# Four-layer graph network: head aggregation in transposed form, straight code, another order

## What is computed

```
h = relu(layernorm(x));  x = x + L0(h): softmax over leaky_relu((h W1)(h W2)^T), masked; times h W3; relu
h = relu(layernorm(x));  x = x + L1(h): graph attention, 4 heads of 64; elu
h = relu(layernorm(x));  x = x + L2(h): the one that the change rewrites:
        Q = h Wq + bq; K = h Wk + bk; V = h Wv + bv        4 heads of 64
        scores = Q K^T / 8, -inf where adj == 0; attn = softmax(scores)
        out = (attn V) Wo + bo; layernorm(out) * gamma + beta
h = relu(layernorm(x));  x = x + L3(h): graph attention, other weights; elu
```

## Time and profile before

| | us |
|---|---|
| median of 3 runs | 3187.79 |
| lowest and highest of them | 3183.66, 3192.85 |
| the profiled execution | 3183.85 |
| its span, first to last instruction | 3182.1 |
| mean granted clock of TensorE, as a share of 2.4 GHz | 0.985 |
| busy: PE, DVE, ACT, POOL | 3035.8, 2168.6, 1629.6, 765.6 |

### The profile page before, as it was taken

The page is one execution under the profiler, slowest core; times in us unless marked ns, Lnnn a source line. Parts: engine busy times, 40 slices in busy tenths (PEclk is TensorE's granted clock), DMA queues, the critical chain, the costliest instruction groups (busy, mean ns, idle before and its releaser), DMA issues.

```text
span 3182.1 us, 85495 instructions
## 1 busy us (share of the span) xinstructions
PE 3035.8 (95%) x35494; PEld 2287.4 (72%) x35494; DVE 2168.6 (68%) x5660; ACT 1629.6 (51%) x3457; POOL 765.6 (24%) x917
## 2 busy tenths in 40 slices
PE   4799999999999999999999999999999999999985
PEld 2577777777777777777777777777777777777754
DVE  3467767766767766767766767766766766766764
ACT  1355455455555545555545555545555545555533
POOL 1222222222222222222222222222222222222221
PEclk8999999999999999999999999999999999999998
DMA  3000000000000000000000000000000000000000
GB/s 75 14 8 9 15 15 15 8 15 9 15 15 16 8 15 8 16 15 15 9 15 8 15 15 15 8 15 9 15 15 16 8 15 8 16 8 8 2 8 14
DMA packets 38468, 43.75 MB, mean 14 GB/s; under 512 B 2496, under 2 KB 37312, under 8 KB 38048
## 3 DMA queue, kind: packets, MB, share of 16 engines
q1 hardware_dynamic: 37552, 36.97, 3.7%
q0 software_dynamic: 496, 0.92, 0.3%
HBM read 21.11 MB, written 16.78 MB: 12 GB/s over the span
## 4 chain that ended last, share of the span: by engine, by line
PE 90%; ACT 4%; DVE 3%; issue 2%; POOL 0%; SPq 0%; DMA 0%; DVEq 0%; POOLq 0%; ACTq 0%
PE ps L895 19%; PE ps L1000 16%; PE ps L901 11%; PE ps L1051 8%; PE ps L931 7%; PE ps L1026 7%; PE ps L952 7%; PE ps L1035 6%; PE ps L985 4%; PE ps L886 3%; PE ps L940 2%; ACT hn L413 1%; ACT qT L539 1%; DVE stats L629 1%; ACT qx L468 0%
## 5 line engine op out<-in xcount | busy, mean ns | idle before, releaser
L730 DVE SCALAR_TENSOR_TENSOR pA<-ps,gval,adjT 128x512 f32<-128x512 f32 x512 | 358.0, 742 | 209.4 <-PE ps L985 209.4
L413 ACT ACTIVATE hn<-xc,nb,rstd 128x256 f32<-128x256 f32 x384 | 208.4, 592 | 327.4 <-DVE nb L646 327.4
L730 DVE SCALAR_TENSOR_TENSOR pB<-ps,gval,adjT 128x512 f32<-128x512 f32 x512 | 354.4, 740 | 1.0 <-PE ps L1000 1.0
L336 POOL TENSOR_SCALAR rstd<-mv 128x4 f32<-128x4 f32 x160 | 36.7, 229 | 1213.9 <-DVE mv L638 1213.9
L1000 PEld LDWEIGHTS ps<-vals,pA 128*64 128x64 f32 x8192 | 251.0, 138 | 82.1 <-issue 77.5
L1000 PEld LDWEIGHTS ps<-vals,pB 128*64 128x64 f32 x8192 | 249.3, 138 | 82.3 <-issue 57.1
L895 PE MATMUL ps<-wgat,hT 128*128 128x264 f32 x1024 | 272.2, 401 | 8.3 <-DVE pB L783 4.2
L1000 PE MATMUL ps<-vals,pA 128*64 128x65 f32 x8192 | 268.7, 224 | 5.7 <-DVE pA L730 5.7
L349 POOL TENSOR_TENSOR vals<-qx,gval 128x256 f32<-128x256 f32 x256 | 153.8, 622 | 497.8 <-ACT gval L480 497.8
L1000 PE MATMUL ps<-vals,pB 128*64 128x65 f32 x8192 | 267.1, 224 | 5.9 <-DVE pB L730 4.3
L361 POOL TENSOR_TENSOR qx<-qx,xc 128x512 f32<-128x512 f32 x128 | 163.2, 1275 | 364.6 <-ACT qx L489 364.6
(11 more groups left out here) (136 smaller groups left out, 6102.6 us busy)
## 6 DMA issues: line engine op xcount, KB each, us to landing
x_in<-in_x SPq DMA_DIRECT2D x32, 512.0 KB, 3.8
out_x<-xc SPq DMA_DIRECT2D x32, 512.0 KB, 4.0
pX<-in_adj SPq DMA_DIRECT2D x1, 1024.0 KB, 5.8
pX<-in_L_gnn_W SPq DMA_DIRECT2D x2, 256.0 KB, 6.5
pA<-in_L_gnn_a POOLq DMA_DIRECT2D x8, 64.0 KB, 11.7
w<-in_L_gnn_W SPq DMA_DIRECT2D x1, 256.0 KB, 8.2
wgat<-in_L_gnn_W SPq DMA_DIRECT2D x1, 256.0 KB, 9.9
wgat<-in_L_gnn_W SPq DMA_DIRECT2D x2, 128.0 KB, 13.4
```

Source lines behind the costliest of these rows:

```text
L413: nc.scalar.activation(hn[s][:, t, :], src[:, t, :], ACT.Identity if norm == "in" else ACT.Relu, bias=nb[s][:, t:t + 1], scale=rstd[s][:, ...
L730: last = nc.vector.scalar_tensor_tensor(out=gat_p[s][h % 2][:, t, :], in0=ps[:, BANK[f"R{g}.{h}"], :], scalar=gval[s][:, 1, t, h:h + 1], i ...
```

## The change

Three things. `slots` has no loop: all 34 slots are written out, for every engine, and semaphore counts are constants. The aggregation of layer 2 is made for two heads at once and transposed: the values (128x64) are the stationary operand, the transposed weights of a key tile for all 512 rows the moving one, one head in each half of the array's columns. Its result has features on partitions, as `o_rows` wants it, so `o_columns` and `o_transposed` are gone. The inverse row sums must then lie along the row: `inverse_sums2` (DVE) takes the reciprocal with each of the two heads' sums repeated 64 times (128x512), `inverse_spread` (PE) transposes it in four blocks, `inverse_out` (ACT) copies it, `norm2` multiplies. And all lists and banks are written anew: `aggregate2` twice instead of four times, `scores2` in other places, `plus_beta` of GpSimd at the end of the slot before. SP's issues are the same ones in the same turns.

```diff
-            slot(Work(0), None, None)
-            slot(Work(1), Work(0), None)
-            with eng.Fori(0, ROUNDS) as i:
-                for j in range(SETS):
-                    slot(Work(j + 2, i), Work(j + 1, i), Work(j, i))
-            slot(None, Work(B - 1), Work(B - 2))
-            slot(None, None, Work(B - 1))
+            for n in range(B + 2):
+                slot(*[Work(n - d) if 0 <= n - d < B else None for d in range(SETS + 1)])
...
+            def inverse_out(w, p):
+                if w is None:
+                    return
+                invp_ready.wait(act, w, p + 1)
+                nc.scalar.copy(kT[w.s][:, p, :], ps[:, BANK[f"RB{p}"], :]).then_inc(inv_ready.sem, 1)
+
...
+            def inverse_sums2(w, p):
+                if w is None:
+                    return
+                s = w.s
+                p2_ready[2 * p].wait(dve, w, NT)
+                p2_ready[2 * p + 1].wait(dve, w, NT)
+                sums = rowsum[s][:, 2 * p:2 * p + 2, :].rearrange("p h t -> p t h")
+                nc.vector.reciprocal(kT[s][:, p, :].rearrange("p (t h d) -> p t h d", t=NT, h=2),
+                                     sums.unsqueeze(3).broadcast_to([P, NT, 2, D])).then_inc(rinv2.sem, 1)
+
+            def norm2(w, p):
+                if w is None:
+                    return
+                agg2_ready.wait(dve, w, p + 1)
+                inv_ready.wait(dve, w, p + 1)
+                nc.vector.tensor_tensor(qT[w.s][:, p, :], ps[:, BANK[f"G2.{p}"], :], kT[w.s][:, p, :],
+                                        ALU.mult).then_inc(oT_ready.sem, 1)
 
...
 
-            def aggregate2(w, h):
-                if w is None:
-                    return
-                s = w.s
-                if h == 0:
+            def inverse_spread(w, p):
+
+                if w is None:
+                    return
+                rinv2.wait(pe, w, p + 1)
+                for t in range(NT):
+                    cols = slice(t * P, (t + 1) * P)
+                    last = nc.tensor.transpose(ps[:, BANK[f"RB{p}"], cols], kT[w.s][:, p, cols], ident[:, :])
+                last.then_inc(invp_ready.sem, 1)
+
+            def aggregate2(w, p):
+
+                if w is None:
+                    return
+                s = w.s
+                if p == 0:
                     v2_ready.wait(pe, w)
-                pT2_act[h].wait(pe, w, 2)
-                pT2_dve[h].wait(pe, w, 2)
-                for t in range(NT):
-                    for j in range(NT):
-                        for half in range(2):
-                            lo, hi = half * HALF, (half + 1) * HALF
-                            last = nc.tensor.matmul(
-                                ps[lo:hi, BANK[f"G2.{h}"], t * D:(t + 1) * D],
-                                probT2[s][h][:, t, j * P + lo:j * P + hi],
-                                vals[s][:, j, h * D:(h + 1) * D],
-                                start=(j == 0), stop=(j == NT - 1))
+                for h in (2 * p, 2 * p + 1):
+                    pT2_act[h].wait(pe, w, 2)
+                    pT2_dve[h].wait(pe, w, 2)
+                for j in range(NT):
+                    for hh in range(2):
+                        h = 2 * p + hh
+                        last = nc.tensor.matmul(
+                            ps[hh * D:(hh + 1) * D, BANK[f"G2.{p}"], :],
+                            vals[s][:, j, h * D:(h + 1) * D],
+                            probT2[s][h][:, :, j * P:(j + 1) * P],
+                            start=(j == 0), stop=(j == NT - 1))
                 last.then_inc(agg2_ready.sem, 1)
 
```

The new lists. Of DVE the beginning and the end of the slot; of ACT the same; of PE all of it (lines without a sign are the same in both):

```diff
+            def slot(a, b, c, d):
+                weights_out2(c, 3, 0); weights_out2(c, 2, 1); statistics(a, 0); weights_out2(c, 3, 2)
+                mean_and_variance(a, 0); inverse_sums2(c, 1); weights_out2(c, 2, 3); gat_max_t(b, 1)
+                shift_of_norm(a, 0); gat_max(b, 1); norm2(c, 1); gat_shift(b, 1)
+                gat_weights(b, 1, 0, 0, 1, 2, 3); o_out(c); gat_weights(b, 1, 1, 0, 1); statistics(c, "in")
...
+                masked_max2(b, 1, 1, 0); masked_max2(b, 1, 1, 1); masked_max2(b, 1, 2, 0)
+                masked_max2(b, 1, 2, 1); gat_out(c, 3, 0); masked_max2(b, 1, 3, 0)
+                pT2p_ready[0].wait(dve, b, 1); weights_out2(b, 1, 0); masked_max2(b, 1, 3, 1)
+                softmax_shift2(b, 1); inverse_sums2(b, 0); weights_out2(b, 0, 1)
+                pT2p_ready[0].wait(dve, b, 3); weights_out2(b, 1, 2); weights_out2(b, 0, 3); norm2(b, 0)
+                gat_out(c, 3, 1)
```

```diff
+            def slot(a, b, c, d):
+                exp2(c, 3, 1); exp2(c, 2, 1); exp2(c, 2, 2); weights_out2(c, 2, 0); exp2(c, 3, 2)
+                q_out(b, 1, 0); exp2(c, 2, 3); exp2(c, 3, 3); weights_out2(c, 2, 2); weights_out2(c, 3, 1)
+                q_out(b, 1, 1); weights_out2(c, 3, 3); normalised(a, 0, 0); normalised(a, 0, 1)
+                inverse_out(c, 1); normalised(a, 0, 2); normalised(a, 0, 3); gat_exp(b, 1)
...
+                elu_min(c, 3, 0); elu_relu(c, 3, 1); elu_exp(c, 3, 0); elu_min(c, 3, 1); exp2(b, 1, 0)
+                exp2(b, 0, 0); exp2(b, 1, 1); exp2(b, 0, 1); exp2(b, 1, 2); v_out(b, 2); exp2(b, 0, 2)
+                weights_out2(b, 0, 0); exp2(b, 1, 3); exp2(b, 0, 3)
+                pT2p_ready[0].wait(act, b, 2); weights_out2(b, 1, 1); h_transposed(a, 1)
+                weights_out2(b, 0, 2); weights_out2(b, 1, 3); inverse_out(b, 0); exp2(b, 2, 0)
+                exp2(b, 3, 0); elu_exp(c, 3, 1)
```

```diff
+            def slot(a, b, c, d):
+                transposed(b, 1, 2)
+                pT2_dve[1].wait(pe, c, 1); weights_transposed2(c, 0, 2); transposed(b, 1, 3)
+                masked2[1].wait(pe, c, 8); weights_transposed2(c, 0, 3)
+                pT2_act[1].wait(pe, c, 1); weights_transposed2(c, 1, 3); inverse_spread(c, 0)
+                q_rows(b, 1, 0); aggregate2(c, 0); weights_transposed2(c, 2, 0); q_rows(b, 1, 1)
+                weights_transposed2(c, 3, 0)
+                oT_ready.wait(pe, c, 1); weights_transposed2(c, 2, 1); weights_transposed2(c, 3, 1)
+                weights_transposed2(c, 2, 2)
+                qx_ready[1].wait(pe, b, 1); q_rows(b, 1, 2); weights_transposed2(c, 3, 2); q_rows(b, 1, 3)
+                pT2_dve[2].wait(pe, c, 1); weights_transposed2(c, 2, 3); weights_transposed2(c, 3, 3)
+                qx_ready[1].wait(pe, b, 2); inverse_spread(c, 1); gat_max_across(b, 1); aggregate2(c, 1)
+                transposed(a, 0, 0); transposed(a, 0, 1); gat_max_spread(b, 1); transposed(a, 0, 2)
+                o_rows(c, 0); transposed(a, 0, 3); o_rows(c, 1); gat_rows(b, 1, 0); o_rows(c, 2)
+                gat_rows(b, 1, 1); o_rows(c, 3); u_columns(a, 0)
+                gP_ready[1].wait(pe, b, 1); v_rows(a, 0, 0)
+                o_ready.wait(pe, c); gat_rows(b, 1, 2); u_columns(a, 1); gat_aggregate(b, 1, 0)
+                scores0(a, 0); gat_aggregate(b, 1, 1); gat_rows(b, 1, 3); scores0(a, 1); v_rows(a, 0, 1)
+                gP_ready[1].wait(pe, b, 3); scores0(a, 2); scores0(a, 3); gat_aggregate(b, 1, 2)
+                gat_aggregate(b, 1, 3)
+                masked0.wait(pe, a, 4); transposed(c, 3, 0); v_rows(a, 0, 2); transposed(c, 3, 1)
+                transposed(c, 3, 2); transposed(c, 3, 3); weights_transposed0(a, 0); v_rows(a, 0, 3)
+                q_rows(c, 3, 0); q_rows(c, 3, 1)
+                pT0_act.wait(pe, a, 1); q_rows(c, 3, 2); weights_transposed0(a, 1); q_rows(c, 3, 3)
+                aggregate0(a, 0); weights_transposed0(a, 2); gat_max_across(c, 3); aggregate0(a, 1)
+                gat_max_spread(c, 3); weights_transposed0(a, 3); aggregate0(a, 2); gat_rows(c, 3, 0)
+                transposed(b, 2, 0); gat_rows(c, 3, 1); transposed(b, 2, 1); aggregate0(a, 3)
+                transposed(b, 2, 2); gat_rows(c, 3, 2); transposed(b, 2, 3); gat_aggregate(c, 3, 0)
+                qk_columns(b, "QT", 0)
+                agg0_norm.wait(pe, a, 4); gat_aggregate(c, 3, 1); gat_rows(c, 3, 3)
+                gnorm[3].wait(pe, c, 1); qk_columns(b, "KT", 0); qk_columns(b, "QT", 1)
                 qk_columns(b, "KT", 1); gat_aggregate(c, 3, 2); scores2(b, 0, 0)
+                kT_ready.wait(pe, b, 2); scores2(b, 0, 1)
+                gnorm[3].wait(pe, c, 3); scores2(b, 1, 0); gat_aggregate(c, 3, 3)
+                masked2[1].wait(pe, b, 2); scores2(b, 0, 2); scores2(b, 0, 3)
+                masked2[0].wait(pe, b, 4); v_rows(b, 2, 0)
+                gnorm[3].wait(pe, c, 4); scores2(b, 1, 1); v_rows(b, 2, 1)
+                masked2[0].wait(pe, b, 6); scores2(b, 1, 2); v_rows(b, 2, 2); weights_transposed2(b, 1, 0)
+                v_rows(b, 2, 3)
+                masked2[1].wait(pe, b, 4); scores2(b, 1, 3)
+                masked2[1].wait(pe, b, 6); weights_transposed2(b, 0, 0); weights_transposed2(b, 1, 1)
+                v2_ready.wait(pe, b); transposed(a, 1, 0); weights_transposed2(b, 0, 1); transposed(a, 1, 1)
+                pT2_act[0].wait(pe, b, 1); weights_transposed2(b, 1, 2)
```

(53 more changed lines are left out.)

124 lines of the change are left out of this document (9 added, 115 removed), and 18 rows, old and new, of the table BANK.

## The result

| | before | changed |
|---|---|---|
| median of 4 runs each, us | 3185.89 | 3334.99 |
| lowest and highest | 3183.66, 3192.85 | 3331.36, 3337.46 |
| span of the profiled execution | 3182.1 | 3335.7 |
| mean granted clock | 0.985 | 0.969 |

The account below looks back on a forecast made before the run. TensorE's (PE) own instruction queue was taken to bound the kernel. From 3183.85 us, 36.0 for branches back and 0.9 a slot (26.1 + 2.7) came off, giving 3119 us; own range 3098 to 3150, 8 in 10 3098 to 3345.

Parts of the forecast that it names:

- The step that failed: DVE's reciprocal of 512 elements was put at 0.69 us, like a multiply; bounds 0.6 to 3.5 us.
- Rival A: DVE's wide reciprocal is slow and PE waits twice a slot: at 3.2 us, time 3332 us; chance 0.29.
- first and second place: PE's waits at `inverse_spread(c, 0)` and `inverse_spread(c, 1)`; forecast 0.15 and 0.45 us, with a slow reciprocal 2.2 and 2.7.
- low clock: After PE idles, its clock is partly at 1.2 GHz: 1.45 us each time, 1.9 us a slot with slow reciprocals.
- Branches back: At the loop's nine branches PE loses 36.0 us together, 4.0 each; straight code saves all of it.
- The transposed aggregation: On PE, two groups of 16 instructions, 3.63 us each, replace four of 64; 1.2 us less a slot.
- rival C: On PE, array halves don't overlap at 512 columns: 6.9 us a group, time 3310 us; chance 0.03.
- `scores2`: On PE, its runs of 12, 8, 12 become 12, 8, 4, 4, 4: 7.90 instead of 7.47 us.
- PE's queue: PE's own instructions in one slot become 0.9 us shorter, from 92.95 to 92.05 us.
- `plus_beta`: On GpSimd, moved behind layer 1's last statistics, it still ends some 10 us before `gat_out` of layer 3.
- Rival D: Finer waits of the new order cost 0.9 us more, leaving only the branches' gain: 3148 us; chance 0.13.
- B: DVE's wide reciprocal takes 4.2 us: slot 103.0 us, time about 3423 us; chance 0.07.

Follow-up runs that it names:

- e5: The changed kernel with ten extra reciprocals and constant multiplies of 4 to 512 elements in DVE's setup; reciprocal of 512 elements 3.34 us.
- e10: The changed kernel with the wide reciprocal for heads 0 and 1 only, a small one with a copy for heads 2 and 3; 3212.13 us, ratio 1.008.
- e9: The changed kernel with the wide reciprocal for heads 2 and 3 only, a small one with a copy for heads 0 and 1; 3239.52 us, ratio 1.0165.
- e4: The changed kernel with 18 and 22 useless transposes put on PE before its two waits for the reciprocals; 3287.26 us, ratio 1.0325.
- e3: The changed kernel with each wide reciprocal taken over 256 of its 512 elements; 3184.97 us, ratio 1.0005.
- e12: e1 with GpSimd's `plus_beta` put back at the head of its slot; 3109.80 us, ratio 0.9766.
- e2: The kernel before with its loop written out and otherwise the same; 3148.59 us, ratio 0.989.
- e1: The changed kernel with each wide reciprocal replaced by one of the eight sums and a copy that repeats them; 3129.66 us, ratio 0.983.
- e13: The changed kernel, wide reciprocals kept, with GpSimd's `plus_beta` back at the head of its slot; 3317.42 us, ratio 1.042.

## Why the prediction was wrong, step by step

**The step that failed** is "By the multiply a reciprocal costs what a copy does, 0.69 ... I take 0.69, since the one-input multiply is the nearest row". It measured 3.34 us. The bounds (0.6 to 3.5) held it, near the upper end. The two rows that the choice rested on, a reciprocal and a multiply of 4 elements with the same step of 0.08 us between starts, could not decide: the difference sought was 0.02 to 0.03 us, the records are no finer than that, and I took "no difference seen" for "no difference". The other evidence, up to 5 ns an element from the same step, came nearer (6.25 measured), but by luck: the constant multiply had the same step, and e5 gives it 0.5 ns an element. The Trainium skill ("VectorE: DVE Perf Modes", First, the fixed hardware budget) gives a repeat count of 8, estimated in the prediction at 4.3 us; the trace has 3.34 us for 512 elements, so the iteration that the page tells of fits the slow rate in kind, and the estimate made from it was high.

**Rival A's working** held in its mechanism, and nearly in its terms:

| term | forecast by A | measured |
|---|---|---|
| reciprocal, us | 3.2 | 3.34 |
| idle of PE at the first and second place | 2.2, 2.7 | 1.99, 2.64 (e10, e9) |
| low clock, us a slot | 1.9 | 1.5 (e4) |
| one low window, us | 1.45 | 1.23 at the first place, 1.67 at the second |
| break-even length of the reciprocal | 1.7 | ratio 1.0005 at 1.74 (e3) |
| slot, us | 100.0 | 99.68 |
| time, us | 3332 | 3335 |

That the last two lines fit so closely is in part luck. In the slot the base was 0.4 us too high (92.95, where e12 has 92.52), the price of the reciprocal 0.2 (5.2 for 4.96, which is 98.15 less 93.19) and the low clock 0.4, while the 0.67 us of `plus_beta` was missing. In the time the slot's 0.3 to 0.4 us too many, some 10 us over 29 slots, made up for the slots outside them, which cost 16 us and not 6. Its rule that a us of reciprocal comes back twice a slot, because DVE stands ahead of PE at both places, is what e3 and e4 show (3.2 us for 1.6); the 0.6 us from which it was to count were 0.25 too few.

**The other steps of the forecast.**
- Branches back: 36.0 us, right (35.6, e2), and nothing took their place.
- The transposed aggregation: 3.63 us for 16 instructions, right (3.59 to 3.65), so rival C is out. Halves of the columns run side by side at 512 columns too: in the timeline of the changed kernel they start in pairs, 0.01 to 0.02 us apart, a pair every 0.43 us.

```profile
1386.76 0.59 PE L1063 MATMUL ps<-pB,vals 128*64 128x512 f32 x1
1386.78 0.59 PE L1063 MATMUL ps<-pX,vals 128*64 128x512 f32 x1
...
1387.19 0.59 PE L1063 MATMUL ps<-pB,vals 128*64 128x512 f32 x1
1387.20 0.59 PE L1063 MATMUL ps<-pX,vals 128*64 128x512 f32 x1
```

- `scores2`: 7.90 us a slot from the runs of 12, 8, 4, 4, 4. In e12, where nothing cuts a run, the records give 7.87; in e1 8.54, of which 0.40 is the wait and 0.27 the cut.
- PE's queue 92.05 us and waits 0.9 make a slot of 92.95. e12 has 92.52, and PE is busy for 92.43 to 92.44 of it, so the queue was 0.4 us longer than I had added up, and the waits are 0.1. Those that I had found at the two places (0.15 and 0.45) are not among the waits of its steady slots. I had taken 0.69 for the reciprocal there; the small one and its copy take 0.19 and 0.43. The queue became shorter by 1.0 us (93.45 busy in e2), near the 0.9 of the forecast.
- `plus_beta` "still ends some 10 us before `gat_out`": true, and the wrong question. The step asked who waits for the moved operation and not whom it disturbs at its new place. Cost 0.67 us a slot, 20 us of time in e1 (3129.66 to 3109.80), 17.6 in the changed kernel (e13). Without it and with a short reciprocal the kernel took 3110 (e12), under the 3119 of the forecast: its slot was 0.43 us too long (29 x 0.43 = 12 us), as two errors, the queue too short and the waits too long, did not quite cancel.
- Rival D (finer waits, 3148) has no support: e1, with PE's wait at `scores2` in it, took 3130 us.
- The chance of faster, 0.58, is a hundredth under its two parts (0.46 and 0.13), and that of slower one under its three; nothing hangs on it.

**What would have decided it beforehand.** Nothing in the trace of before fixes the reciprocal's rate, and the chance of 0.36 for A and B together admitted that. But the value should not have gone by the likeness of another operation's fixed part. The only thing at hand that spoke of a rate was the iteration that the Trainium skill ("VectorE: DVE Perf Modes", First, the fixed hardware budget) names, and it pointed to A and B.

## What to carry to other kernels

An instruction of a few elements shows only its fixed part. When a change widens such an operation, its rate has to come from a wide instance of the same operation. A reciprocal of repeated values is better computed small and repeated with a copy (0.19 + 0.43 us for 3.34). When an operation is moved, ask also what runs on the other engines at its new place: GpSimd's add there cost as much as two thirds of a per cent of the time (20 us of 3130) without anyone waiting for its result. The sign to look for is a small DVE operation that is many times longer in places and ends with a GpSimd one.
